# A graph layer on one core: in the gather, the fourth sum of a step moved behind the shifts

## The chip, the cores and the metric

The kernel runs on one core of one Trainium2 chip. The metric is the time on the device in microseconds (us), the median of several runs. Engines: TensorE (PE in the rows; PEld is its weight load), VectorE (DVE), ScalarE (ACT), GpSimd (POOL), SyncE (SP).

## The reference, cut to what matters

The whole layer is layernorm, a graph attention over 106,250 edges, a mixing branch, a residual sum and eight experts. The change touches only the attention's last part:

```
xn = _layernorm(x, axis=-1)
h = xn @ W_layer.T + b_layer
v = leaky_relu(a1[row] + a2[col])
m = segment_max(v, row);  ev = exp(v - m[row]);  s = segment_sum(ev, row)
out = segment_sum((ev / s[row])[:, None] * h[col], row)
```

The kernel needs, for every edge, the row of h of its other end, and adds these rows, weighted, into the sum of the edge's own node, with a running maximum so that the exponents stay small.

## The kernel before, in words

The program has four stages that follow one another: tables and the mixing inputs (to about 374 us in the profile), the gather (about 374 to 1710 us), the routing, the experts. The change lies in the gather.

The edges are sorted and cut into 878 tiles of 128 edges. One step of the gather handles four tiles (G = 4, `q` runs over them), and there are 220 steps plus a tail of five. The loop is written out (`steady`), and each engine has its own list of step bodies. The engines are held together by semaphores alone, so the order of the work on one engine is the order of its instructions, and a wait in the middle of a step holds all that stands behind it on that engine. Step i works on several tiles at different depths:

- GpSimd (L1146) fetches the rows of step i: four indirect DMAs, one after another. Step i may start when `pe_step` has reached i - 3.
- VectorE begins its step i with L1299 (a small clamp of the scores) and L1302 (`hot`, one 128x512 comparison, for step i). It reads four column numbers into registers (L1307). Then it waits for `pe_step >= i`, and then come, in order: sum 0 (`add(i, j, 0)`, L1288), small operations of the exponents (L1266), a copy (L1316), sum 1, L1269, the maximum over the transposed tile (L1322), L1272, sum 2, the scan (L1330), a copy (L1336), `lin` (L1338), in two steps of every four one 128x256 operation of the mixing branch (L1343 or L1348), sum 3, and then the shifts: L1352 (signals `shift_ready`), L1358, L1363 (signals `dm_ready`). L1352 waits for `lin`, L1358 for L1352, L1363 for L1358.
- A sum takes a 128x257 product out of PSUM and adds it to an accumulator in SBUF: `acc = acc * alpha + psum`. It signals `acc_done`. The sums of step i belong to the tiles of step i - 5.
- ScalarE makes `masked` for the transposes (L1219), the weights (L1232), the sign of the transposed tile (L1239) and small exponentials (L1227, L1243).
- TensorE's step i is: in two steps of every four a product of the mixing branch (L1161, or L1166 with L1168), four small products (L1184, for tile group i - 2; they wait for `shift_ready` i - 1), four products of 257 columns (L1192, for tile group i - 4, q = 0 to 3), and four transposes (L1200, for tile group i). The product q of L1192 goes into the PSUM bank that sum q of the group before has to have left: it waits for that sum's `acc_done`. The last transpose signals `pe_step` = i + 1.

So one loop closes over two engines: sum 3 of VectorE's step i releases TensorE's product 3 of its step i; behind that stand the transposes; these signal `pe_step` = i + 1; and VectorE's sum 0 of step i + 1 waits for it, as GpSimd's fetches of step i + 4 do.

Of the kernel before, what the change touches and what calls it, by code (L numbers as in the profile page):

```python
# [60 lines left out]
def build(nc, x, src, dst, w_h, w_hT, b_h, w_a, b_a, w_qkv, w_vT, b_qkv, w_out, b_out, b_cols, w_router, w13, w2, out):  # L61
    assert (E + NBK * 127) // P <= USED <= GT <= SW and 0 < REST <= G and ROWS6 < PAD0 and (2 * N + NE * 127) // P <= MT
    ctx = ExitStack()
    with ctx:
        def sem(name):
            return ctx.enter_context(nc.semaphore(name))
# [113 lines left out]
        def S(name):  # L180
            name = again.get(name, (name, 0))[0]
            if name not in s:
                s[name] = sem(name)
            return s[name]

        def due(value):

            return not isinstance(value, int) or value > 0
# [127 lines left out]
        def ds(i, n=1):  # L316
            return slice(i, i + n) if isinstance(i, int) else bass.ds(i, n)
# [800 lines left out]
        def steady(eng, step, lag):  # L1118
            for i in range(NG + lag):
                step(i, i % RING, i // RING)  # L1120
# [6 lines left out]
        def live(i, lag, n=NG):  # L1127

            return not isinstance(i, int) or 0 <= i - lag < n
# [117 lines left out]
        def gather_vector(dve):  # L1247
# [26 lines left out]
            def add(i, j, q, columns):  # L1274

                if not live(i, 5):
                    return
                t = i - 5
                if t * G + q >= USED:
                    return  # L1280
                if t == 0 and q == 0:
                    dve.wait_ge(S("acc_cleared"), 1)
                if q == 0:
                    dve.wait_ge(S("alpha_ready"), t + 1)
                if due(t * G + q):
                    dve.wait_ge(S("acc_done"), t * G + q)
                here = acc[:, bass.ds(columns[q], C + 1)]
                v.scalar_tensor_tensor(here, here, alpha[(j - 5) % RING][:, q:q + 1], psum[4 + q][:, 0:C + 1],  # L1288
                                       ALU.mult, ALU.add).then_inc(S("acc_done"), 1)

            def step(i, j, k):
                columns = None
# [13 lines left out]
                if live(i, 5):  # L1306
                    _, columns = nc.values_load_multi_w_load_instructions(  # L1307
                        bt_i[0:1, ds((i - 5) * G, G)], engines=(dve.engine,), min_val=0, max_val=(NT - 1) * TW,
                        skip_runtime_bounds_check_because="the table holds first columns of buckets")
# [36 lines left out]
                if m is not None:  # L1346
                    dve.wait_ge(S("part_ready"), m + 1)
                    v.tensor_tensor(mix_b[m % MS], psum[3][:, C:2 * C], mix_b[m % MS], ALU.add).then_inc(S("half_ready"), 1)  # L1348
                add(i, j, 3, columns)
                if live(i, 1):  # L1350
                    dve.wait_ge(S("lin_steps"), t + 1)
                    v.scalar_tensor_tensor(lb[b][:, G + 1:2 * G + 1], lin[:, :], SLOPE, lin[:, :], ALU.mult, ALU.max)\  # L1352
                        .then_inc(S("shift_ready"), 1)

                    dve.wait_ge(S("shift_ready"), t + 1)
                    if due(t):
                        dve.wait_ge(S("dm_ready"), t)
                    v.tensor_tensor(dm0[:, :], lb[b][:, G:2 * G], lb[b][:, G + 1:2 * G + 1], ALU.subtract)\  # L1358
                        .then_inc(S("dm_steps"), 1)
                    dve.wait_ge(S("dm_steps"), t + 1)  # L1360
                    if due(t):
                        dve.wait_ge(S("alpha_ready"), t)
                    v.tensor_tensor(dm[:, :], dm0[:, :], same[:, ds(t * G, G)], ALU.mult).then_inc(S("dm_ready"), 1)  # L1363

            steady(dve, step, 5)


# [502 lines left out]
        @block.vector  # L1870
        def _(dve):
            o = Order(dve, "v_steps")
            first_vector(dve, o)
            mix_vector(dve, o)
            tables_vector(dve, o)
            phase(dve, 1)
            gather_vector(dve)
            phase(dve, 2)
            route_vector(dve, o)
            phase(dve, 3)  # L1880
            experts_vector(dve)
# [61 lines left out]
```

## Time and profile before

| | |
|---|---|
| median of 3 runs | 2658.95 us (2657.84 to 2660.27) |
| the profiled execution | 2658.12 us, span 2656.4 us |
| TensorE, busy share of the span | 85% |
| VectorE | 66% |
| ScalarE, GpSimd | 48%, 48% |
| mean granted TensorE clock | 0.882 of full |

The span is the time from the first to the last instruction of the core; the run's time lies 1.7 us above it. The busy shares are averages over four stages with different limits. A row of the timeline gives the start, the duration, the engine and the line; what stands in square brackets is how long the engine had been idle before it, and what ended that. "remote" there means that the wait ended at a moment for which the profile shows no instruction that had just finished.

### The profile page before, as it was taken

How to read it: one execution, taken by the hardware profiler on the slowest of the kernel's cores; microseconds unless marked ns; L12 is line 12 of the kernel's file. 1: busy time of each engine (PE TensorE's matmuls, PEld its weight loads, DVE VectorE, ACT ScalarE, POOL GpSimd, SP SyncE). 2: the span in 40 equal slices, each digit the busy share in tenths (PEclk: the TensorE clock that was granted, in tenths of full speed). 3: DMA queues.
4: the chain of work that ended last, by engine and by line, in shares of the span. 5: the costliest groups of instructions: out<-in, count | busy, mean ns of one | idle time of the engine just before them, and what ended most of it. 6: DMA issues, size and time to landing. Idle time of an engine off the chain costs nothing.

```text
span 2656.4 us, 44842 instructions
## 1 busy us (share of the span) xinstructions
PE 2251.5 (85%) x12642; PEld 1855.9 (70%) x12659; DVE 1741.7 (66%) x5623; ACT 1284.6 (48%) x3862; POOL 1264.2 (48%) x1271
## 2 busy tenths in 40 slices
PE   3789847777778787877788887779999999999997
PEld 2566635555556565655557665578999999999997
DVE  8677747777777777777777776777555555555553
ACT  7666645555555555555555555555222222222221
POOL 0000045666666666666666666102444444444443
PEclk8899967889987878889987777759999999999999
DMA  2344333434443444444444434583222222222222
GB/s 80 91 136 120 123 90 90 112 106 112 114 111 106 112 114 111 109 110 113 112 108 110 112 109 87 81 259 129 35 35 37 35 35 35 35 37 34 36 35 27
DMA packets 141977, 237.83 MB, mean 90 GB/s; under 512 B 29546, under 2 KB 101066, under 8 KB 140970
## 3 DMA queue, kind: packets, MB, share of 16 engines
q0 software_dynamic: 65664, 143.64, 24.3%
q1 hardware_dynamic: 76074, 91.34, 10.7%
q8 instruction: 110, 1.80, 0.3%
q14 instruction: 129, 1.06, 0.1%
HBM read 182.34 MB, written 52.53 MB: 88 GB/s over the span
## 4 chain that ended last, share of the span: by engine, by line
PE 51%; DVE 21%; issue 13%; another core or an unknown queue 6%; DVEq 4%; ACT 3%; DMA 1%; POOL 0%; SPq 0%; ACTq 0%; POOLq 0%
PE psum L1705 20%; PE psum L1740 10%; DVE arena L1288 9%; PE psum L1192 7%; DVEq L1307 4%; PE psum L521 3%; PE psum L1200 2%; PE psum L1184 2%; DVE arena L1299 1%; DVE arena L1330 1%; PE psum L500 1%; PE psum L1470 1%; DVE arena L1358 1%; DVE arena L1352 1%
## 5 line engine op out<-in xcount | busy, mean ns | idle before, releaser
L1146 POOL DMA_INDIRECT arena<-table,arena x878 | 864.1, 984 | 473.8 <-issue 254.4
L1192 PE MATMUL psum<-arena 128*128 128x257 f32 x1756 | 659.1, 496 | 240.0 <-DVE arena L1288 135.4
L1192 PEld LDWEIGHTS psum<-arena 128*128 128x128 f32 x1756 | 343.9, 231 | 456.0 <-issue 356.9
L1288 DVE SCALAR_TENSOR_TENSOR arena<-arena,psum 128x257 f32 x878 | 420.3, 479 | 316.7 <-remote 179.4
L1705 PE MATMUL psum<-arena 128*128 128x128 f32 x4620 | 551.7, 276 | 0.6 <-ACT arena L1762 0.6
L1705 PEld LDWEIGHTS psum<-arena 128*128 128x128 f32 x4620 | 542.4, 192 | 6.7 <-issue 0.9
L1837 POOL DMA_INDIRECT out<-arena x105 | 169.7, 1616 | 383.3 <-ACT arena L1769 380.4
L1219 ACT ACTIVATE arena<-arena 128x128 f32<-128x128 bf16 x880 | 280.9, 390 | 117.0 <-DVE arena L1302 68.8
L1740 PE MATMUL psum<-arena 128*128 x1260 | 290.7, 379 | 0.8 <-ACT arena L1769 0.8
L1232 ACT ACTIVATE arena<-arena 128x128 f32<-128x128 bf16 x880 | 281.2, 391 | 7.1
L1184 PEld LDWEIGHTS psum<-arena 128*128 128x128 f32 x1760 | 249.8, 213 | 24.3 <-issue 18.6
L1740 PEld LDWEIGHTS psum<-arena 128*128 128x128 f32 x1260 | 230.9, 190 | 30.0 <-issue 1.2
L1184 PE MATMUL psum<-arena 128*128 128x2 f32 x1760 | 234.0, 255 | 19.1 <-ACT arena L1239 15.9
L1227 ACT ACTIVATE arena<-arena 128x4 f32<-128x4 f32 x220 | 45.1, 205 | 406.3 <-DVE arena L1272 259.0
L1815 DVE TENSOR_TENSOR arena<-psum,arena 128x512 f32<-128x512 f32 x105 | 72.7, 692 | 240.0 <-ACT arena L1776 240.0
L1769 ACT ACTIVATE arena<-psum,arena 128x256 f32<-128x256 f32 x105 | 49.9, 475 | 370.5 <-PE psum L1740 370.5
L1200 PEld LDWEIGHTS psum<-arena 128*128 128x128 f32 x880 | 141.3, 173 | 58.1 <-issue 33.4
L1200 PE MATMUL psum<-arena 128*128 128x128 f32 x880 | 167.4, 323 | 16.9 <-issue 14.9
L462 POOL COPY arena<-arena 128x2 f32<-128x2 f32 x49 | 21.1, 430 | 314.2 <-DVE arena L784 314.2
L1686 POOL DMA_INDIRECT arena<-normalised,arena x105 | 100.7, 959 | 145.5 <-DMA gates<-arena 112.7
L1803 DVE COPY arena<-arena 128x2560 f32 x105 | 156.9, 1494 | 10.0 <-ACT arena L1760 1.5
L1302 DVE TENSOR_TENSOR arena<-arena 128x512 bf16<-128x512 bf16 x220 | 151.1, 687 | 0.5 <-issue 0.5
(346 smaller groups left out, 3125.8 us busy)
## 6 DMA issues: line engine op xcount, KB each, us to landing
mix_inputs<-arena SPq DMA_DIRECT2D x147, 128.0 KB, 2.2
arena<-table,arena POOLq DMA_INDIRECT x878
arena<-in_x SPq DMA_DIRECT2D x98, 128.0 KB, 2.8
arena<-mix_inputs SPq DMA_DIRECT2D x49, 256.0 KB
arena<-in_w SPq DMA_DIRECT2D x6, 1364.0 KB, 6.5
out<-arena SPq DMA_DIRECT2D x50, 128.0 KB, 1.9
table<-arena SPq DMA_DIRECT2D x49, 129.0 KB, 2.3
arena<-mix_inputs SPq DMA_DIRECT2D x49, 128.0 KB, 2.6
```

The source lines that it names most:

```text
L1146: pool.indirect_dma_start(rows_in[j][:, q * TW:(q + 1) * TW], None, table_d[:, :], bass.IndirectOffsetOnAxis(ap=col_all[:, t:t + 1], axis=0))\
L1184: last = mm(psum[2 + b][:, 2 * q:2 * q + 2], member[b][:, q * P:(q + 1) * P], lb[b][:, q:q + G + 2:G + 1], start=True, stop=True)
L1192: last = mm(psum[4 + q][:, 0:C + 1], weight[b][:, q * P:(q + 1) * P], rows_in[g][:, q * TW:q * TW + C + 1], start=True, stop=True)
L1200: last = nc.tensor.transpose(psum[b][:, q * P:(q + 1) * P], masked[b][:, q * P:(q + 1) * P], ident[:, :])
L1219: a(masked[j % 2][:, q * P:(q + 1) * P], hot[j][:, q * P:(q + 1) * P], ACT.Copy, scale=a2s[j % 2][:, q:q + 1]).then_inc(S("masked_ready"), 1)
L1232: a(weight[b][:, q * P:(q + 1) * P], hot[(j - 3) % RING][:, q * P:(q + 1) * P], ACT.Copy, scale=wexp[b][:, q:q + 1]).then_inc(S("weight_re ...
L1288: v.scalar_tensor_tensor(here, here, alpha[(j - 5) % RING][:, q:q + 1], psum[4 + q][:, 0:C + 1], ALU.mult, ALU.add).then_inc(S("acc_done"), 1)
L1302: v.tensor_tensor(hot[j].rearrange("p (q r) -> p q r", q=G), iota_b.unsqueeze(1).to_broadcast([P, G, P]), lane_row[:, ds(i * G, G)].unsque ...
L1705: last = mm(to, weights(c), xst[i % 2][:, c * P:(c + 1) * P], start=(c == 0), stop=(c == 1))
L1740: last = mm(psum[6][:, 0:C], gg[i % 2][:, c * P:(c + 1) * P], w2_sb[:, bass.ds(e * (FC * C) + c * C, C)], start=(c == 0), stop=(c == FC - 1))
L1803: v.tensor_copy(to[:, :, 0:10 * P].rearrange("p k (m n) -> p k m n", m=2), of[:, :, :, FL:F])
L1837: pool.indirect_dma_start(out[:, :], bass.IndirectOffsetOnAxis(ap=row_i[:, i:i + 1], axis=0), yo[i % 2][:, :], None, compute_op=ALU.add).t ...
```

## The change

VectorE's sum 3 of a step (`add(i, j, 3, columns)`) moves from in front of the shifts to the end of the step. No instruction is added or removed. Nothing of the other engines' programs changes, nor does any semaphore or the value that anyone waits for.

```diff
@@ -1346,7 +1346,6 @@
                 if m is not None:
                     dve.wait_ge(S("part_ready"), m + 1)
                     v.tensor_tensor(mix_b[m % MS], psum[3][:, C:2 * C], mix_b[m % MS], ALU.add).then_inc(S("half_ready"), 1)
-                add(i, j, 3, columns)
                 if live(i, 1):
                     dve.wait_ge(S("lin_steps"), t + 1)
                     v.scalar_tensor_tensor(lb[b][:, G + 1:2 * G + 1], lin[:, :], SLOPE, lin[:, :], ALU.mult, ALU.max)\
@@ -1361,6 +1360,7 @@
                     if due(t):
                         dve.wait_ge(S("alpha_ready"), t)
                     v.tensor_tensor(dm[:, :], dm0[:, :], same[:, ds(t * G, G)], ALU.mult).then_inc(S("dm_ready"), 1)
+                add(i, j, 3, columns)
```

## Rows read from the trace of the kernel before

**Rows 1.** Windows, gather: us, engines' busy (x), granted clock, DMA share, GB/s.

```profile
409.00:1690.00 1281.00, 1041.48 (x4725) 781.80 (x4726) 926.66 (x3736) 724.37 (x2352) 833.36 (x846) 0.84 0.42 108
```

**Rows 2.** Waits, whole run: total us, times, longest.

```profile
DVE arena L1288 <- remote: 179.4, 85, 3.1
POOL arena L1146 <- remote: 161.2, 86, 2.4
```

**Rows 3.** Timeline, one step without a mixing operation, lower clock at its end.

```profile
1106.23 0.48 DVE L1288 SCALAR_TENSOR_TENSOR arena<-arena,psum 128x257 f32 x1 [2.34 <-remote]
...
1108.37 0.22 DVE L1330 TENSOR_TENSOR_SCAN arena<-arena 128x4 f32<-128x4 f32 x1
...
1108.63 0.22 DVE L1338 SCALAR_TENSOR_TENSOR arena<-arena 128x4 f32<-128x4 f32 x1
1108.77 0.48 DVE L1288 SCALAR_TENSOR_TENSOR arena<-arena,psum 128x257 f32 x1
...
1109.16 0.16 DVE L1352 SCALAR_TENSOR_TENSOR arena<-arena 128x4 f32<-128x4 f32 x1
...
1109.63 0.23 DVE L1299 TENSOR_SCALAR arena<-arena 128x4 f32<-128x4 f32 x1
...
1110.45 1.06 PE L1200 MATMUL psum<-arena 128*128 128x128 f32 x4
...
1111.64 0.48 DVE L1288 SCALAR_TENSOR_TENSOR arena<-arena,psum 128x257 f32 x1 [1.19 <-issue]
```

**Rows 4.** Timeline, the next step, full clock at its end.

```profile
1114.18 0.48 DVE L1288 SCALAR_TENSOR_TENSOR arena<-arena,psum 128x257 f32 x1
...
1115.31 0.60 PE L1200 MATMUL psum<-arena 128*128 128x128 f32 x4
...
1118.19 0.48 DVE L1288 SCALAR_TENSOR_TENSOR arena<-arena,psum 128x257 f32 x1 [2.33 <-remote]
```

**Rows 5.** Timeline, a step with a mixing operation.

```profile
1121.12 0.47 DVE L1288 SCALAR_TENSOR_TENSOR arena<-arena,psum 128x257 f32 x1
...
1121.50 0.16 DVE L1352 SCALAR_TENSOR_TENSOR arena<-arena 128x4 f32<-128x4 f32 x1
...
1121.98 0.23 DVE L1299 TENSOR_SCALAR arena<-arena 128x4 f32<-128x4 f32 x1
```

**Rows 6.** Timeline, VectorE: the first sum of five steps that follow one another.

```profile
973.98 0.48 DVE L1288 SCALAR_TENSOR_TENSOR arena<-arena,psum 128x257 f32 x1 [2.31 <-remote]
...
979.71 0.48 DVE L1288 SCALAR_TENSOR_TENSOR arena<-arena,psum 128x257 f32 x1 [1.11 <-issue]
...
986.04 0.48 DVE L1288 SCALAR_TENSOR_TENSOR arena<-arena,psum 128x257 f32 x1 [1.52 <-PE psum L1200]
...
990.71 0.48 DVE L1288 SCALAR_TENSOR_TENSOR arena<-arena,psum 128x257 f32 x1 [0.44 <-issue]
...
998.06 0.48 DVE L1288 SCALAR_TENSOR_TENSOR arena<-arena,psum 128x257 f32 x1 [3.06 <-remote]
```

**Rows 7.** The sums that start between 421 us and 1670.3 us.

```profile
L1288 DVE SCALAR_TENSOR_TENSOR arena<-arena,psum x832: 468/480/485, 421.1 to 1666.4; 128x257 f32 x167
```

**Rows 8.** GpSimd's fetches: duration in ns min/median/max, first and last start.

```profile
L1146 POOL DMA_INDIRECT arena<-table,arena x878: 941/949/1484, 354.2 to 1677.1; - x176
```

**Rows 9.** Timeline, first sums of a step, four steps apart; the transposes ahead.

```profile
1670.43 0.48 DVE L1288 SCALAR_TENSOR_TENSOR arena<-arena,psum 128x257 f32 x1 [2.35 <-PE psum L1200]
...
1689.09 0.60 PE L1200 MATMUL psum<-arena 128*128 128x128 f32 x4
1690.09 0.48 DVE L1288 SCALAR_TENSOR_TENSOR arena<-arena,psum 128x257 f32 x1 [0.44 <-PE psum L1200]
```

**Rows 10.** Windows, the same columns, over the two steps from 975.7 us.

```profile
975.70:985.80 10.10, 9.77 (x32) 7.68 (x32) 7.41 (x31) 6.85 (x22) 6.30 (x7) 0.50 0.46 114
```

**Rows 11.** Timeline, PE, the transposes at the end of that stretch.

```profile
984.50 1.06 PE L1200 MATMUL psum<-arena 128*128 128x128 f32 x4
```

**Rows 12.** L1363's idle before it: who ended it, us, times.

```profile
  DVE arena L1358: 17.1, 21
```

## The prediction

> **What bounds the gather now.** I began with the windows, to see whether an engine is full in the stage: in the 1281 us of the steady gather no engine is full. TensorE has 1041 us, VectorE 927, GpSimd 833, ScalarE 724, at a mean granted clock of 0.84 [rows 1]. So the stage goes by waits. The list of waits says which: VectorE's sums and GpSimd's fetches have the same long wait, 85 and 86 times, about 2 us each, and both wait for `pe_step` [rows 2].
>
> The timeline shows that steps come in pairs. After a long wait (2.34 us) a step starts at 1106.23; the next starts 5.41 us later, 0.13 us behind the end of the transposes (1110.45 + 1.06) [rows 3]. In that next step the transposes end at 1115.91, but VectorE gets its signal only for 1118.19, 2.28 us later [rows 4]. One step of a pair is therefore paced by the loop sum 3, product 3, transposes, sum 0; in the other that loop is done early and something else holds the signal.
>
> What holds it keeps its own time. From 973.98 the pair is 5.73 + 6.33 = 12.06 us; from 986.04 it is 4.67 + 7.35 = 12.02 [rows 6]. One first step was 1.06 us longer than the other, and the second gave back all of it but 0.04. Over the stage: from the first sum at 421.1 to the one at 1670.43 stand 832 sums, which are 208 steps or 104 pairs, so 1249.3 / 104 = 12.01 us for a pair [rows 7, 9]. When GpSimd's last fetches go out (start of the last 1677.1 [rows 8]) it is gone: the four steps from 1670.43 to 1690.09 take 19.66 us, 9.83 for two [rows 9]. So the pace belongs to the time in which fetches run. I can't name the mechanism; the sum below uses only that it is there.
>
> **The change, part by part.** Nothing is removed or added; one instruction of 0.48 us changes places, with its register work, and issues no DMA. No instruction of SP or POOL is passed.
>
> *Step without a mixing operation (half of them).* Before: `lin` 1108.63, sum 3 1108.77, L1352 1109.16, next step's L1299 1109.63 [rows 3]. L1352 needs `lin`'s result. With sum 3 gone from between them it starts at the distance that another such pair shows, scan to `lin`, 1108.63 - 1108.37 = 0.26. That is 0.53 - 0.26 = 0.27 us earlier. Sum 3 then starts where L1299 would have, 0.47 behind L1352: 1108.63 + 0.26 + 0.47 = 1109.36, which is **0.59 us later**. L1299 follows 0.39 behind (the distance of sum 3 to L1352 before): 1109.75, 0.12 later. This bubble is the price on VectorE, because sum 3 had filled the wait on `lin`.
>
> *Step with one.* The mixing operation fills the wait on `lin`. L1352 takes sum 3's place (1121.12), and sum 3 that of L1299, 0.48 behind: 1121.60, **0.48 later**; L1299 comes at 1121.99 against 1121.98 [rows 5].
>
> *Who gains.* `shift_ready` and `dm_ready` come 0.27 to 0.38 us earlier. L1184 waits for the first and ScalarE's L1243 for the second. TensorE reaches L1184 only behind L1192 and L1200 of its step, and both hang on sum 3, so the earlier signal buys nothing. I book 0; the bound below is 0 too, since no row shows L1352 as what L1184's engine lacked in a steady step.
>
> *Who loses.* Product 3 of L1192 waits for sum 3, and behind it on TensorE stand its two passes, the four transposes, and then all of the next step; `pe_step` comes from the last transpose, and VectorE's sum 0 and GpSimd's next four fetches wait for that. At the lower clock the array is partly the limit: from the end of sum 3 (1109.25) to the end of the transposes are 2.26 us, at full clock 1114.66 to 1115.91, 1.25 us [rows 3, 4]. Bounds for what reaches the signal: nothing, if the array is the limit throughout, and the whole 0.59 or 0.48. I take the whole, since at full clock nothing but the chain lies there.
>
> *The pair.* First step: 5.41 becomes up to 6.00. Second step: another 0.59. Together 1.18 us, and 0.96 in a pair with mixing operations. The cover is the held signal: 2.28 us, less the 0.13 that a signal needs anyway, is 2.15 us [rows 3, 4]. So these pairs stay at 12.01 us: cost 0. Without the cover they cost 1.18 and 0.96.
>
> *Where the cover is thin.* From 975.7 to 985.8 the granted clock is 0.50, the 1.2 GHz level, and the pair began behind a wait of 2.31 us [rows 6, 10]. There the transposes end at 985.56 and sum 0 starts at 986.04 [rows 6, 11]: 0.48, so cover 0.35. This is a mixing pair: 0.96 - 0.35 = 0.61 us over. How many are like it? A mean clock of 0.84 is 32% of the time at the lower level [rows 1], part of it in steps like the one of rows 3, whose pair has its cover in the second step. Bounds 0 and 0.32 x 104 = 33 pairs. I take 8: such a pair, once longer, drifts against the clock's changes and out of this state. 8 x 0.61 = 4.9 us.
>
> *The ends.* The last five steps with shifts run when no fetches do. There the transposes end at 1689.69, 0.40 us before sum 0 [rows 9], so 0.27 are slack. 0.59 - 0.27 = 0.32 us a step: 1.6 us.
>
> *Sum*: 4.9 + 1.6 = 6.5 us on the profiled 2658.12 us, 0.8 us under the median. On the median: 2665.4, and I say **2665 us**. Its own range is 2657 to 2673 (0 to 20 thin pairs, and 2 us).
>
> **A rule of the Trainium skill.** The row: in one step sum 0 starts 0.13 us behind the transposes' end, in the next 2.28 us behind it, with the same four instructions [rows 3, 4]. The Trainium skill, page "Perfetto Trace Analysis", section "Tensor Engine Instruction (MATMUL, LD_WEIGHTS)", says that the reported end of a matmul is an estimate, and that the signal goes out only when PSUM has acknowledged the writes. By that rule the 2.28 us could be a fixed tail of TensorE's own, no cover, and the change would cost what the first rival below does. The trace speaks against it, since the same tail is 0.13 in every other step.
>
> **Rivals.**
> *The held signal follows the transposes at a fixed distance.* Then each step moves by the whole delay: 104 pairs x (1.18 + 0.96) / 2 = 111 us, so about 2770. For it: the wait is 2.31, 2.34 and 2.33 us in three places [rows 3, 4, 6]. Against: 3.06 us after a short first step, and two pairs equal to 0.04 us [rows 6]. Chance 0.12.
>
> *VectorE's own small waits hold sum 3.* L1363 waited 17.1 us in 21 places for L1358, an instruction of its own engine that takes 0.16 us: 0.8 us each [rows 12]. Now sum 3 stands behind L1352, L1358 and L1363. A delay of 0.8 on top of 1.18 is 1.98, just under the cover of 2.15; two such in one step break it. If a third of the pairs ran over by 0.5 us: 104 / 3 x 0.5 = 17 us more, about 2682. For it: all shifts move to a later place in the pair, where these delays are. Chance 0.18.
>
> *Faster: the pace of the pair is bound to GpSimd's fetches being disturbed.* A fetch takes 949 ns in the median but up to 1484 [rows 8]; eight of them are 7.6 us of a pair's 12.01. If an overlap with L1302 stretches one by 0.5 us and L1302's 0.12 us shift removes it in half the pairs, the pace falls: 52 x 0.5 = 26 us, about 2633. It decides only if the pair's pace hangs on the fetches' own durations. Against: L1302 doesn't move in mixing steps. Chance 0.06.
>
> *The cover holds*: 0.64, likelier in the form with some microseconds of leak than with none.
>
> **How the numbers follow.** No change can be told within 0.2%, 5.3 us. The cover case is split: 0.37 within, 0.27 over. The fetch rival gives faster 0.06; I give 0.01 more for luck with the clock. The fixed tail 0.12 and the small waits 0.18, of which 0.03 stay within. Faster 0.07, same 0.40, slower 0.53. The range leaves out the fixed tail and most of the faster case: 2655 to 2692.
>
> **What would show it.** In the changed kernel: L1352 0.26 us behind `lin` in a step without mixing; sum 3 ends 0.59 and 0.48 later in its step; first steps of pairs near 5.9 and 5.3 us; second steps shorter by as much; pairs still 12.0 us; the remote wait in front of L1288 down from 179 us to about 179 - 85 x 1.07 = 88. It is wrong if pairs become 13 us (fixed tail), if idle in front of L1358 or L1363 grows to more than 50 us (small waits), or if pairs fall under 11.9.

## The result and the profile after

| | before | after |
|---|---|---|
| median | 2659.1 us (4 runs, 2657.84 to 2660.27) | 2676.62 us (4 runs, 2675.05 to 2678.13) |
| profiled execution, span | 2656.4 us | 2673.3 us |
| from sum 0 of step 5 to sum 0 of step 219 | 1280.9 us | 1296.0 us |

The ratio is 1.0067, with a 95% interval of 1.0051 to 1.0083: slower by 17.5 us. Of the 16.9 us between the two spans 15.1 lie between sum 0 of step 5 and sum 0 of step 219. Another 2.4 lie in the five steps behind that, up to sum 0 of step 224 (18.85 us before, 21.29 after), and the rest of the program is 0.6 us shorter.

The windows of the kernel after, over the stretch of [rows 1]: the engines do the same work at nearly the same clock (0.83 against 0.84).

```profile
409.00:1690.00 1281.00, 1035.42 (x4663) 775.20 (x4664) 932.34 (x3686) 703.67 (x2321) 836.12 (x844) 0.83 0.42 108
```

The waits of the kernel after, which answer to [rows 2]:

```profile
DVE arena L1288 <- PE psum L1200: 196.3, 131, 4.1
POOL arena L1146 <- PE psum L1200: 154.8, 107, 14.1
...
DVE arena L1288 <- remote: 96.5, 40, 3.0
...
POOL arena L1146 <- remote: 71.9, 40, 2.1
```

The remote waits fell from 179.4 us in 85 places to 96.5 in 40, against a forecast of about 88. That these two numbers are so near is partly luck: the forecast had 85 shorter waits, and the row has 40 that are longer on average (2.41 us against 2.11). The starts and ends themselves say it better. I call a signal *held* where sum 0 starts more than 0.75 us behind the end of the transposes. This happens 91 times in the kernel before, by 2.31 us on average, and 76 times in the kernel after, by 1.55. Less 0.13 us each, that is 198 us before and 108 after: the cover is being used up. VectorE's timeline of one step without a mixing operation, after, beside [rows 3]:

```profile
507.10 0.22 DVE L1338 SCALAR_TENSOR_TENSOR arena<-arena 128x4 f32<-128x4 f32 x1
507.36 0.18 DVE L1351 SCALAR_TENSOR_TENSOR arena<-arena 128x4 f32<-128x4 f32 x1
507.57 0.17 DVE L1357 TENSOR_TENSOR arena<-arena 128x4 f32<-128x4 f32 x1
507.77 0.16 DVE L1362 TENSOR_TENSOR arena<-arena 128x4 f32<-128x4 f32 x1
507.88 0.48 DVE L1288 SCALAR_TENSOR_TENSOR arena<-arena,psum 128x257 f32 x1
508.28 0.22 DVE L1299 TENSOR_SCALAR arena<-arena 128x4 f32<-128x4 f32 x1
```

L1351 (the old L1352) starts 0.26 us behind `lin` (507.36 - 507.10), sum 3 0.78 behind it (0.14 before: +0.64), L1299 1.18 behind it (1.00 before: +0.18). The source view of the last shift in the kernel after, against [rows 12]:

```profile
  DVE arena L1357: 1.1, 4
```

**Where the 15 us arise.** I took the start of sum 0 of every step and formed 104 pairs from step 5 on. Of these, 94 are within 0.1 us of 12.01 before; after, 52, with a median of still 12.03, but 27 are over 12.2 (4 before), up to 13.46. Put otherwise, from one held signal to the next lie in the kernel before two steps (12.0 us, 76 times) or four (24.05 us, 14 times), but never three. After, they are two steps (12.03 us, 40 times), three (median 18.2 us, 18 times), four (24.3 us, 14 times), twice five and once six. What such a gap has over 6.0 us a step adds up to 7.6 us in those of three steps, 4.8 in those of four, 2.9 in those of five and 0.7 in those of two: 16.0 us. In the kernel before the same sum is 1.3 us; the difference of 14.7 is the loss.

One of the gaps of five, in the kernel after. VectorE's first sums of three steps:

```profile
504.70 0.48 DVE L1288 SCALAR_TENSOR_TENSOR arena<-arena,psum 128x257 f32 x1 [1.64 <-PE psum L1200]
...
510.69 0.48 DVE L1288 SCALAR_TENSOR_TENSOR arena<-arena,psum 128x257 f32 x1 [1.60 <-issue]
...
518.17 0.48 DVE L1288 SCALAR_TENSOR_TENSOR arena<-arena,psum 128x257 f32 x1 [3.10 <-PE psum L1200]
```

TensorE in the same steps, and the windows of the two steps (columns as in [rows 1]):

```profile
509.50 1.06 PE L1200 MATMUL psum<-arena 128*128 128x128 f32 x4
510.35 1.92 PE L1161 MATMUL psum<-arena 128*128 128x256 f32 x4
512.06 1.71 PE L1184 MATMUL psum<-arena 128*128 128x2 f32 x8
513.62 3.77 PE L1192 MATMUL psum<-arena 128*128 128x257 f32 x8
517.19 0.84 PE L1200 MATMUL psum<-arena 128*128 128x128 f32 x4
```

```profile
504.70:510.70 6.00, 4.74 (x17) 3.14 (x17) 4.29 (x18) 3.34 (x11) 4.16 (x4) 0.73 0.47 143
510.70:518.20 7.50, 7.50 (x27) 6.27 (x26) 4.29 (x18) 3.33 (x11) 4.14 (x4) 0.54 0.32 85
```

The first step takes 5.99 us. In the second TensorE is busy for all of its 7.50 us, at a granted clock of 0.54, nearly all of it the 1.2 GHz level; its transposes end at 518.03 and sum 0 follows 0.14 us later, with no held signal left to hide anything: 13.47 us for the two. What fills this step is TensorE's own product of the mixing branch (L1161, 1.92 us at this clock) on top of its usual work. The kernel after has eight steps of this kind, 7.1 to 7.5 us at a granted clock of 0.53 to 0.56, each with such a product (L1161 or L1168) in it. They are the only steps over 6.8 us that end without a held signal, and each stands behind a step of 5.98 or 5.99 us. The eight gaps that contain them lose 10.0 of the 16.0 us. In the kernel before none of the 34 steps at a clock of 0.60 or less has a mixing product of TensorE in it for more than 0.5 us. The other kind of overrun is a held signal that has slipped into the other step of the pair. VectorE's first sums in the kernel after:

```profile
1168.18 0.48 DVE L1288 SCALAR_TENSOR_TENSOR arena<-arena,psum 128x257 f32 x1 [2.40 <-remote]
...
1173.22 0.48 DVE L1288 SCALAR_TENSOR_TENSOR arena<-arena,psum 128x257 f32 x1 [0.66 <-PE psum L1200]
...
1180.24 0.48 DVE L1288 SCALAR_TENSOR_TENSOR arena<-arena,psum 128x257 f32 x1 [2.38 <-remote]
...
1186.42 0.48 DVE L1288 SCALAR_TENSOR_TENSOR arena<-arena,psum 128x257 f32 x1 [1.56 <-PE psum L1200]
```

The held signals are 12.06 us apart. The step behind the second, at a clock of 0.50, takes 6.18 us, and the one behind that 5.98; neither is held. The third, 6.03 us, is, and the three come to 18.2.

### The profile page after: what moved, and what is told of

It is laid out like the page before. It is cut to its first block, busy times and chain, and to the rows that moved or that the text cites. A ratio compares the mean times of both kernels' runs of the same rounds, so it can differ in the third digit from the quotient of the medians.

```text
span 2673.3 us, 44842 instructions
## 1 busy us (share of the span) xinstructions
PE 2258.2 (84%) x12642; PEld 1859.9 (70%) x12659; DVE 1760.2 (66%) x5623; ACT 1272.4 (48%) x3862; POOL 1269.1 (47%) x1271
## 4 chain that ended last, share of the span: by engine, by line
PE 58%; DVE 19%; issue 11%; ACT 5%; another core or an unknown queue 4%; DVEq 2%; DMA 1%; POOL 0%; ACTq 0%; SPq 0%; POOLq 0%
PE psum L1705 19%; PE psum L1740 10%; PE psum L1192 10%; DVE arena L1288 8%; PE psum L1200 5%; PE psum L521 3%; PE psum L1184 2%; ACT arena L1232 2%; DVE arena L1302 2%; DVEq L1307 1%; PE psum L500 1%; PE psum L1470 1%; ACT arena L592 1%; PE psum L1490 1%
## 5 line engine op out<-in xcount | busy, mean ns | idle before, releaser
L1146 POOL DMA_INDIRECT arena<-table,arena x878 | 869.7, 991 | 482.8 <-issue 242.0
L1288 DVE SCALAR_TENSOR_TENSOR arena<-arena,psum 128x257 f32 x878 | 421.9, 481 | 343.3 <-PE psum L1200 196.3
L1184 PE MATMUL psum<-arena 128*128 128x2 f32 x1760 | 240.3, 258 | 18.6 <-ACT arena L1239 18.1
```

The source lines that it names most:

```text
L1146: pool.indirect_dma_start(rows_in[j][:, q * TW:(q + 1) * TW], None, table_d[:, :], bass.IndirectOffsetOnAxis(ap=col_all[:, t:t + 1], axis=0))\
L1184: last = mm(psum[2 + b][:, 2 * q:2 * q + 2], member[b][:, q * P:(q + 1) * P], lb[b][:, q:q + G + 2:G + 1], start=True, stop=True)
```

## The experiments

A job is one batch of runs on one chip. All ratios are to runs of the kernel before in the same job. The kernel before itself came out at two levels, and the levels decide how every number is read: 2658 to 2659 us in the first measurement and in the job of E7 to E9, 2446 to 2449 us in the jobs of E1 to E4, of E5 and E6, of E10 and E11, and of E12. E1 to E4 and E7 to E9 ran on one and the same chip, so the level isn't the chip's. I call the jobs at 2659 us *held* and those at 2446 us *free*.

| | kernel | job | ratio to before (95%) |
|---|---|---|---|
| | after, first measurement | held | 1.0067 (1.0051 to 1.0083) |
| E1 | late in mixing steps alone | free | 1.0028 (1.0017 to 1.0039) |
| E2 | late in the other steps alone | free | 1.0061 (1.0045 to 1.0076) |
| E3 | sum 3 early | free | 1.0147 (1.0132 to 1.0162) |
| E4 | 0.48 us more in front of sum 3 | free | 1.0250 (1.0233 to 1.0266) |
| E5 | after | free | 1.0127 (1.0110 to 1.0144) |
| E6 | before, for its trace | free | one run, 2446.04 us |
| E7 | after, transposes ahead of product 3 | held | 1.0035 (1.0022 to 1.0048) |
| E8 | before, transposes ahead of product 3 | held | 1.0000 (0.9991 to 1.0009) |
| E9 | after, dummy products | held | 1.0117 (1.0102 to 1.0132) |
| E10 | before, three fetches of four | free | 0.9949 (0.9932 to 0.9966) |
| E11 | as E4 | free | 1.0258 (1.0241 to 1.0275) |
| E12 | as E7, three fetches of four | free | 0.9735 (0.9714 to 0.9755) |

For the free jobs this table carries most of the reading. It gives the median length in us of the steps that ran wholly at full clock, from the starts of sum 0 in each trace, by their place in the cycle of four (31 to 51 steps for each number; for E3 the first has 13 and the last 17). Steps 1 and 2 have no mixing operation, steps 3 and 4 have one.

| | 1 | 2 | 3 | 4 |
|---|---|---|---|---|
| before (E6) | 4.67 | 4.67 | 5.07 | 5.15 |
| after (E5) | 5.03 | 5.03 | 5.30 | 5.24 |
| E1 | 4.67 | 4.67 | 5.30 | 5.23 |
| E2 | 5.03 | 5.03 | 5.06 | 5.14 |
| E3 | 5.01 | 5.01 | 5.28 | 5.47 |
| E4 | 5.06 | 5.06 | 5.45 | 5.40 |
| E10 | 4.72 | 4.67 | 5.06 | 5.15 |
| E12 | 4.64 | 4.61 | 4.86 | 4.95 |

**E1 and E2: half of the change.**

```diff
-                add(i, j, 3, columns)
+                late = (i % 4 in (0, 3)) == True
+                if not late:
+                    add(i, j, 3, columns)
...
+                if late:
+                    add(i, j, 3, columns)
```

The last two lines stand at the end of the step; E2 has `False` for `True`.

Expected of E1: 

> The kernel before, with sum 3 at the end of the step only in the steps with a mixing operation (both steps of every second pair); nothing is left out. Theory (held signal covers the delay; what leaks is a pair whose second step TensorE runs at the lower clock, so that the transposes end after the signal's moment): these pairs stay at 12.0 us where the clock is high, and the whole is 4 to 9 us over the kernel before, somewhat under half of the 17.5 us of the full change, since the delay here is 0.96 us a pair against 1.18. Rival, fixed tail: 52 x 0.96 = +50 us. Rival, the leak does not come from the delay but from the bubble behind lin in the other steps: 0.

Expected of E2: 

> The kernel before, with sum 3 at the end of the step only in the steps without a mixing operation; nothing is left out. Theory: +8 to +13 us (somewhat over half of 17.5), and with the run before this one it adds up to about 17.5. Rival, fixed tail: 52 x 1.18 = +61 us. Rival, bubble behind lin: the whole +17.5.

Both were written for a held job and met a free one. At full clock each half lengthens its own steps, by 0.36 us without a mixing operation and by 0.23 and 0.08 with one, and leaves the others alone. The whole times, +0.28% and +0.61%, are less than these steps add up to; E5 takes that up.

**E3: the opposite move.**

```diff
                 add(i, j, 2, columns)
+                add(i, j, 3, columns)
                 if live(i, 1):
...
-                add(i, j, 3, columns)
```

Expected: 

> The kernel before, with sum 3 right behind sum 2, in front of the scan, in every step: the opposite move; nothing is left out. The scan, the copy and lin that it passes start 0.13 to 0.5 us apart, so sum 3 starts up to 0.9 us earlier, unless product 3 is not ready. Theory: the pairs stay at 12.0 us; only what leaks already in the kernel before can be won, 0 to 8 us faster. Rival, fixed tail: 104 x 1.2 = 125 us faster at most, some 60 or more in any case. Rival, the scan and lin that come later cost something of their own: slower.

36 us slower, against my expectation in sign. Timeline of E3 in a step without a mixing operation (sums 2 and 3, scan, `lin`, first shift):

```profile
1002.43 1.09 DVE L1288 SCALAR_TENSOR_TENSOR arena<-arena,psum 128x257 f32 x2
...
1003.43 0.22 DVE L1331 TENSOR_TENSOR_SCAN arena<-arena 128x4 f32<-128x4 f32 x1
...
1003.69 0.22 DVE L1339 SCALAR_TENSOR_TENSOR arena<-arena 128x4 f32<-128x4 f32 x1
1003.95 0.16 DVE L1352 SCALAR_TENSOR_TENSOR arena<-arena 128x4 f32<-128x4 f32 x1
```

and of the kernel before in a free job (E6; sum 2, scan, `lin`, sum 3):

```profile
1001.89 0.48 DVE L1288 SCALAR_TENSOR_TENSOR arena<-arena,psum 128x257 f32 x1
1002.29 0.22 DVE L1330 TENSOR_TENSOR_SCAN arena<-arena 128x4 f32<-128x4 f32 x1
...
1002.54 0.23 DVE L1338 SCALAR_TENSOR_TENSOR arena<-arena 128x4 f32<-128x4 f32 x1
1002.68 0.48 DVE L1288 SCALAR_TENSOR_TENSOR arena<-arena,psum 128x257 f32 x1
```

In E6 the scan starts 0.40 us behind sum 2. Two sums would take 0.80, and in E3 they take 1.00: sum 3 stands 0.20 us longer, which fits a wait for its product. The first shift starts 0.26 us behind `lin`, where sum 3 started 0.14 behind it: another 0.12, the bubble that the prediction had for the changed kernel. Together that is 0.32 of the 0.34 us by which these steps are longer. The granted clock over 409 to 1480 us is lower too, 0.90 against 0.94, and what share of the 36 us that has isn't separated. So sum 3 is too early in one place and too late in the other, and the place that it had was the best of three in a free job.

**E4: the delay without the new order.** One more operation of the form of a sum, into a spare tile, in front of sum 3.

```diff
+                if live(i, 5):
...
+                    v.scalar_tensor_tensor(dummy_out[:, 0:C + 1], zeros[:, 0:C + 1], alpha[(j - 5) % RING][:, 3:4],
+                                           psum[7][:, 0:C + 1], ALU.mult, ALU.add).then_inc(S("dummy_steps"), 1)
                 add(i, j, 3, columns)
```

Expected: 

> The kernel before, with one more operation of VectorE in front of sum 3 of every step, of the same form and size as a sum (0.48 us), into a spare tile; no order changes and nothing is left out. It delays sum 3 by 0.48 us (0.96 us a pair) and everything behind it as well, L1299 of the next step too. Theory: the leak depends on the delay of sum 3 alone, so +12 to +18 us. Rival, fixed tail: +100 us. Rival, the leak comes from the new order of shifts and sum: near 0 to +5.

+62 us, in a free job, far over the 12 to 18 that I expected for a held one. Timeline of E4 (L1354 is the added operation, L1289 the sums):

```profile
996.38 0.48 DVE L1289 SCALAR_TENSOR_TENSOR arena<-arena,psum 128x257 f32 x1 [1.09 <-PE psum L1201]
...
998.92 0.48 DVE L1354 SCALAR_TENSOR_TENSOR arena<-arena,psum 128x257 bf16<-128x257 f32 x1
999.31 0.48 DVE L1289 SCALAR_TENSOR_TENSOR arena<-arena,psum 128x257 f32 x1
```

It costs 0.39 us of VectorE's queue (999.31 - 998.92), and the steps are longer by 0.39, 0.39, 0.38 and 0.25. Nearly all of it arrives: in a free job VectorE's own queue sets the full-clock step of the kernel before. It doesn't set the mean step alone, as the fetches in the next section show.

**E5 and E6: both kernels in a free job.**

Expected of E5: 

> The changed kernel once more, since the chip of the four runs before this one ran the kernel before in 2445.7 us instead of 2659, with no wait of the kind that held every pair at 12.0 us. Theory: on a chip without the held signal the change costs about the sum of the two half changes there, 0.28% + 0.61% = 0.9% (22 us), and its steps are paced by the loop of sum 3, product 3 and transposes; on a chip with the held signal 0.67% (17 us), as first measured. Rival: without the cover the whole delay counts, 111 us (4.5%).

Expected of E6: 

> The kernel before, unchanged, for its trace on this chip. If this chip is like the one of the last runs: no remote wait in front of L1288, no fixed pace of a pair, steps of 5.0 us, 2446 us. If it is like the first: 2659 us, about 85 remote waits of 2 us, pairs of 12.0 us.

2480.1 us against 2448.3. The trace of E6 has no remote wait on L1288 or L1146 at all. Its timeline:

```profile
998.02 0.48 DVE L1288 SCALAR_TENSOR_TENSOR arena<-arena,psum 128x257 f32 x1
...
998.88 0.23 DVE L1299 TENSOR_SCALAR arena<-arena 128x4 f32<-128x4 f32 x1
...
999.15 0.60 PE L1200 MATMUL psum<-arena 128*128 128x128 f32 x4
1000.14 0.48 DVE L1288 SCALAR_TENSOR_TENSOR arena<-arena,psum 128x257 f32 x1 [0.44 <-PE psum L1200]
...
1004.81 0.48 DVE L1288 SCALAR_TENSOR_TENSOR arena<-arena,psum 128x257 f32 x1 [0.39 <-PE psum L1200]
```

and that of E5:

```profile
1042.97 0.48 DVE L1288 SCALAR_TENSOR_TENSOR arena<-arena,psum 128x257 f32 x1 [0.66 <-PE psum L1200]
...
1046.13 0.48 DVE L1288 SCALAR_TENSOR_TENSOR arena<-arena,psum 128x257 f32 x1
1046.53 0.35 DVE L1299 TENSOR_SCALAR arena<-arena 128x4 f32<-128x4 f32 x1
...
1047.27 0.60 PE L1200 MATMUL psum<-arena 128*128 128x128 f32 x4
...
1048.00 0.48 DVE L1288 SCALAR_TENSOR_TENSOR arena<-arena,psum 128x257 f32 x1 [0.66 <-PE psum L1200]
```

Before, the transposes end at 999.75, 0.39 us ahead of sum 0; that is 0.26 more than a signal needs, and VectorE is the pace. After, they end at 1047.87 and sum 0 comes 0.13 behind: the loop over TensorE is the pace. The delay of sum 3 is 0.59 to 0.64 us, the slack 0.26, and 0.36 us come through. The halves add up to 0.89%, as I expected of the whole, but the whole is 1.27%.

A second limit stands beside VectorE's in a free job: GpSimd's fetches. From E6:

```profile
999.76 0.94 POOL L1146 DMA_INDIRECT arena<-table,arena  x1 [0.30 <-issue]
...
1004.75 0.95 POOL L1146 DMA_INDIRECT arena<-table,arena  x1 [0.30 <-issue]
```

Four fetches take 4.99 us, since 0.30 us lie between one and the next. In E6 95% of the fetches between 409 and 1430 us start within 1.3 us of the one before, so GpSimd is issuing almost without a pause, and the mean step is 5.07 us. Full-clock steps of 4.67 us are possible only while the fetches are some steps ahead. In E1 the share is still 95%, in E2 91%, in E5 84%. A delay on the other engines is therefore hidden in part until it has used up this limit. E10, which takes a fetch away, puts the limit at 0.5% of the kernel before. If each half hides 0.5% under this limit, and the whole hides 0.5% once and not twice, the whole should cost 0.89% + 0.5% = 1.4%; it cost 1.27%. That is an estimate that fits, not a test.

**E7 and E8: take the transposes out of the loop.** TensorE's transposes of a step move in front of its product 3, and `pe_step` comes from product 3.

```diff
                     for q in range(REST if t == NG - 1 else G):
+                        if q == G - 1 and live(i, 0):
+                            transposes(i, j)
                         pe.wait_ge(S("weight_ready"), t * G + q + 1)
...
-                if live(i, 0):
+                elif live(i, 0):
+                    last = transposes(i, j)
```

Expected of E7: 

> The changed kernel, with TensorE's four transposes of a step in front of product 3 of L1192 in place of behind it; pe_step then comes from product 3; nothing is left out. The transposes need only masked, which is ready some 3.8 us before they start. On a chip without the held signal the changed kernel's full-clock steps without mixing are 5.03 us against 4.67 before, with sum 0 0.13 us behind the end of the transposes. Theory: the loop of sum 3, product 3, transposes, sum 0 has become the pace, so that taking 0.60 us of transposes out of it gives VectorE its own pace back, 4.67 to 4.80 us a step; the whole falls by 20 us or more against the changed kernel and stands within 15 us over the kernel before. Rival: VectorE's own order (the bubble behind lin) makes the 5.03; then the steps stay at 5.0. On a chip with the held signal: within 6 us of the kernel before.

Expected of E8: 

> The kernel before with the same edit on TensorE alone; nothing is left out. Theory: VectorE paces its full-clock steps (4.67 us, sum 0 0.40 us behind the transposes, a slack of 0.27), so the edit gives nothing there and little in all, 0 to 10 us faster, from the steps in which the clock is low. Rival: if the loop over TensorE is the pace in the kernel before as well, 0.3 us or more a step, 60 us.

This job was held. For the changed kernel the loss is halved, 8.8 us in place of 17.5 (expected: within 6); for the kernel before the edit gives nothing, since its loop lay under cover already. Measured behind the end of product 3, which now gives the signal, the held signals in E7 are again two steps apart (68 gaps, median 12.01 us) or four (18), never three: the slips are gone. What remains is of another kind. Timeline of E7 (L1294 are the sums, L1203 the products):

```profile
1176.62 0.48 DVE L1294 SCALAR_TENSOR_TENSOR arena<-arena,psum 128x257 f32 x1
...
1180.11 0.48 DVE L1294 SCALAR_TENSOR_TENSOR arena<-arena,psum 128x257 f32 x1 [2.28 <-PE psum L1203]
```

```profile
1178.78 1.20 PE L1203 MATMUL psum<-arena 128*128 128x257 f32 x2 [2.69 <-remote]
```

Sum 3 ends at 1177.10; product 3, which waits for it, starts at 1178.78. So a signal of VectorE's (`acc_done`) is held up here too, 1.68 us, and product 3 then needs 1.20 us at the lower clock. Where something still has to be done behind the held signal, it can cost. The trace has ten such waits in front of product 3, and seven of them lie in the thirteen pairs that are over 12.2 us (up to 13.1); three lie in pairs of about 12.05, and six of the thirteen have none. So this is a part of what remains, not shown to be all.

**E9: keep TensorE from standing idle.**

```diff
+                    for _ in range(4):
+                        mm(psum[2 + b][:, 2 * G:C], ones_g[:, :], vo_parts[:, 2 * G:C], start=True, stop=True)
```

Expected: 

> The changed kernel with four dummy bf16 products of 248 columns behind L1184 in every step, into columns that nobody reads; they keep TensorE from standing idle there and do no work of the reference. Nothing is left out. Theory: what the lower clock costs is won back where TensorE waits anyway: no steps of 6 us at the lower clock, granted clock near 1, and the whole some 5 to 15 us under the changed kernel. Rival: the dummies (0.4 us a step at full clock) lie in the loop themselves: up to 0.4 x 215 = 86 us slower.

The granted clock over the gather rose from 0.83 to 0.90 (windows of E9),

```profile
409.00:1690.00 1281.00, 1030.75 (x5459) 780.78 (x5458) 925.26 (x3651) 697.58 (x2299) 831.97 (x836) 0.90 0.40 107
```

and the kernel became slower than the changed one, 1.0117 against 1.0067. The steps at the lower level did not go away, and a mixing step at that level is also longer by the dummies: there are second steps of 7.4 to 8.2 us at clocks of 0.54 to 0.58. This neither proves nor refutes that the lower clock is the cause of the leak; it shows that these dummies, put into the loop, cost more than the clock that they buy. I had expected a gain of 5 to 15 us on the changed kernel.

**E10, E11 and E12: fetches, the delay once more, and the loop in a free job.** E10 and E12 fetch three tiles of four:

```diff
-                    for q in range(REST if i == NG - 1 else G):
+                    for q in range(G if i < RING else 3):
```

Expected of E10: 

> The kernel before, with three of the four fetches of each step from step 8 on; the fourth tile of a step uses the rows that its buffer had from steps 0 to 7, so the output is of other rows for a quarter of the tiles. Where the signals are held (the kernel before at 2659 us): if the held signal counts the fetches, 12.0 us for eight, six give 9.0 us, less than the 9.7 to 10.4 us that the engines need, and the time falls to about 2446 us. Rival: it is a period of its own; the pairs stay at 12.0 and the time at 2659. Where they are not held (2446 us): no change beyond 10 us, since GpSimd has slack there.

Expected of E11: 

> The same kernel as the fourth: one more operation of VectorE (0.48 us) in front of sum 3 of every step, no order changed. It cost 62 us where no signal is held. Theory: where the signals are held, the cover of 2.15 us a pair hides the 0.96 us, and only the overruns at the lower clock remain: +8 to +20 us on 2659. Rival: the cover hides only what the new order moves; then +60 us again. Where no signal is held: +60 us as before.

Expected of E12: 

> The changed kernel with the transposes in front of product 3 and with three of four fetches a step from step 8 on (the fourth tile of a step uses old rows). Which of two questions it answers depends on whether signals are held on this chip now. Not held (the kernel before at 2446 us): the full-clock steps without mixing, 5.03 us in the changed kernel and 4.67 in the one before (the latter with three fetches too), tell whether the loop over TensorE had become the pace. Theory: yes, 4.67 to 4.80 us, and about 2446 us in all; rival, VectorE's bubble behind lin makes them: 5.03. Held (the kernel before at 2658 us): if the held signal counts fetches, pairs of 9.0 us at most from it, so about 9.6 to 10.4 from the engines, 2450 us; rival, a period of its own: pairs stay at 12.0 and 2666 us.

All three were aimed at the held signal and met free jobs, so whether it counts fetches stays open. E11 repeats E4 (1.0258 and 1.0250). E10 shows that a quarter fewer fetches gives 0.5%, 12 us, in a free job and leaves the full-clock steps nearly as they were. I had written that GpSimd has slack there; it has almost none. E12 settles what paces the changed kernel's full-clock steps: with the transposes out of the loop the changed kernel's steps fall from 5.03 to 4.61 us, forecast 4.67 to 4.80. Timeline of E12 (L1294 sums, L1305 the old L1299, L1203 products):

```profile
990.44 0.48 DVE L1294 SCALAR_TENSOR_TENSOR arena<-arena,psum 128x257 f32 x1 [0.22 <-PE psum L1203]
...
993.62 0.48 DVE L1294 SCALAR_TENSOR_TENSOR arena<-arena,psum 128x257 f32 x1
994.02 0.22 DVE L1305 TENSOR_SCALAR arena<-arena 128x4 f32<-128x4 f32 x1
...
994.25 0.67 PE L1203 MATMUL psum<-arena 128*128 128x257 f32 x2 [0.32 <-DVE arena L1294]
995.05 0.48 DVE L1294 SCALAR_TENSOR_TENSOR arena<-arena,psum 128x257 f32 x1 [0.22 <-PE psum L1203]
```

From sum 3 to the next sum 0 are 1.43 us, against 1.87 in E5 and 2.12 in E6. The whole is 2384.3 us, where I had expected about 2446. It is 2.65% under the kernel before, but this isn't what the two orders are worth. The mean step of E12 is 4.79 us, and four fetches a step take GpSimd 5.0 us. An estimate of the best case with all fetches: 214 steps x 0.21 = 45 us more, about 2430 us, which is 0.8% under the kernel before. The granted clock is higher as well, 0.97 over 409 to 1480 us against 0.94 in E6. E7's kernel, which has all fetches, was measured in a held job alone, where it is 0.35% slower than before; a version that beats the kernel before at both levels was not shown.

## Why the prediction was right or wrong

I forecast 2665 us and slower by over 0.2% as the likeliest sign; it became 2676.6, inside the range, and outside the 2657 to 2673 of the case that I held likeliest. The mechanism, a cover that hides the delay except where it is thin, was the right one; the term for the thin places was too small.

- *Sum 3 0.59 and 0.48 us later, L1299 0.12.* Right in kind: 0.64 for sum 3 and 0.18 for L1299 in the step shown; the slope in the free jobs agrees (0.36 through a slack of 0.26, where I had 0.32 through 0.27).
- *The bubble on VectorE.* Its 0.12 us costs nothing that I can see: in E12, which has the bubble, the step is 4.61 us, not above the 4.67 of E6.
- *The cover holds the pair at 12.01 us, cost 0.* Right for 52 of 104 pairs to 0.1 us and for the median (12.03). First steps at the lower clock are 5.98 us, with mixing at full clock 5.30.
- *Where the cover is thin: 8 pairs at 0.61 us, 4.9 us.* This is the step that failed, in size. The lost time is some 15 us: eight gaps that lose 1.1 to 1.5 us each and 19 longer than two steps that lose 0.1 to 0.4. That I had eight pairs and the trace has eight heavy gaps is chance; they aren't the same pairs. I priced one pair with the lower clock in both steps and argued that such a pair drifts out of its state. Instead the overruns come in two sizes. In most of the small ones two steps of 5.7 to 6.3 us, at least one of them mostly at the lower clock, stand one behind the other and pass 12.01 together. In the eight large ones a first step of 5.99 us is followed by one at the lower clock with a mixing product of TensorE, 7.1 to 7.5 us, a kind of step that my sum didn't have. Where the transposes end behind the moment of the held signal, the signal slips by a step. There are 18 gaps of three steps, none before; in 13 of them the first two steps pass 12.01 us together, and in the other five they take 11.1 to 11.8, so what moves the signal there stays open. My own upper bound was 33 pairs, and it held 27 that overran.
- *The ends: 1.6 us.* The last three steps are 15.10 us after and 14.35 before, +0.25 us a step against the 0.32 forecast. Right in kind. The five steps behind them take another 2.4 us, which my sum didn't have.
- *Without the cover 1.18 and 0.96 us a pair, 111 us in all.* Wrong, as E5 shows: without held signals the change costs 32 us. The slack in front of sum 0 takes 0.26 us of each delay at full clock, which I had counted for the ends and not here; a part goes into the limit of the fetches; and steps at the lower clock without a VectorE mixing operation are not longer (5.99 us in E6, a median of 5.72 in E5, at a clock of 0.60 or less).
- *Fixed tail.* Refuted. Pairs stay at 12.0, and in the free jobs sum 0 follows the transposes by 0.13 us wherever the loop is the pace. By the rule of the Trainium skill, page "Perfetto Trace Analysis", section "Tensor Engine Instruction (MATMUL, LD_WEIGHTS)", the signal waits for PSUM's acknowledgement; by the reported ends the trace of E5 leaves at most 0.13 us for that here.
- *VectorE's own small waits.* Refuted: 1.1 us in 4 places in front of the last shift, where there were 17.1 in 21.
- *Faster by undisturbed fetches.* Nothing of it was seen at either level. My reading of the row was wrong too: eight fetches aren't 7.6 us of a pair but 10.0, since 0.30 us lie between two of them.

What isn't shown is that the lower clock alone causes the overruns, nor why it falls on other steps in the changed kernel: the trace shows it in them, E7 shows that a shorter loop removes the slips and half of the loss, and E9 failed to separate the two.

## What to carry to other kernels

A wait that hides a delay is worth only what is left of it in the worst step, not in the mean one: price the steps at the lower clock one after another over several steps, since one late step moves the start of the next and can push the hidden wait itself out of place. An operation that releases another engine's next work belongs where its input has just arrived; before that it stalls its own queue (E3, +1.5%), after that it lengthens the loop (+0.7 to +1.3%). Where the loop is the pace, look on the other engine for work that doesn't depend on the signal and stands behind it (E12), and count the next limit, gaps between instructions included, before you hope for the gain (the fetches).

## What the runs showed of the hardware

- The same kernel on the same chip took 2446 us in one job and 2658 us in another, every run of the kernel before at its job's level (2443 to 2452, and 2654 to 2659). From sum 0 of step 5 to that of step 219 are 1280.9 us held and 1085.8 free (E6), 195 of the 212 us; another 18 lie ahead of step 5, where the held trace has one remote wait of 18.9 us. A held pair takes 12.01 us, the free ones 9.74 us and, with mixing operations, 10.40 (means, E6).
- At the slow level, the signals of TensorE (`pe_step`) reach their waiters 2.3 us behind the transposes in the kernel before, at moments 12.0 us apart, and one of VectorE's (`acc_done`, E7) came 1.68 us late. In no free trace is there one such wait.
- GpSimd's indirect fetches start 1.25 us apart at best, 0.95 us of work and 0.30 us between, at both levels.
- Traces of the held jobs also lack records: 154 of the 225 signals of `pe_step` that E6 has are in the trace of the kernel before, and 11,272 arrivals of DMA transfers against 26,983. Every timed run here comes with a span and a clock from the recorder, so whether the recording itself delays the signals, and what sets the level of a job, stays open.
